# Releasing the next batch's work every fifteenth attention step instead of every step

## The reference

```python
xn = _layernorm(x, axis=-1)
q1 = (xn @ W1_q.T).reshape(B, T, H, 4); q2 = (xn @ W2_q.T).reshape(B, T, H, 4)
L_q = exterior(q1, q2)            # 6 normalized 2x2 minors for each head
L_k = exterior(k1, k2)            # the same of the keys
scores = jnp.einsum('bqhc,bkhc->bhqk', L_q, L_k @ _J6.T) * 6.0 ** (-0.5)
attn = jax.nn.softmax(jnp.where(causal, scores, -jnp.inf), axis=-1)
v = (xn @ W_v.T + b_v).reshape(B, T, H, 64)
out = jnp.einsum('bhqk,bkhd->bqhd', attn, v).reshape(B, T, D) @ W_out.T + b_out
out_real = xn_real @ W_real.T - xn_imag @ W_imag.T + bias_real
out_imag = xn_real @ W_imag.T + xn_imag @ W_real.T + bias_imag
return x + out + jnp.concatenate([out_real, out_imag], axis=-1)
```

## Time and profile before

| | |
|---|---|
| median of 3 runs | 4868.14 us (4857.08 to 4872.81) |
| the profiled execution | 4846.63 us, span of its slowest core 4845.6 us |
| spans of the 8 cores | 4806.8 to 4845.6 us |
| mean granted PE clock, core 7 | 0.658 of full speed |
| busy: PE, DVE, ACT | 59%, 29%, 30% of the span |

### The profile page before, as it was taken

The page is one execution under the profiler, slowest core; times in us unless marked ns, Lnnn a source line. Parts: engine busy times, 40 slices in busy tenths (PEclk is TensorE's granted clock), DMA queues, the critical chain, the costliest instruction groups (busy, mean ns, idle before and its releaser), DMA issues.

```text
span 4845.6 us, 35963 instructions; the slowest of 8 cores (4806.8 to 4845.6 us)
## 1 busy us (share of the span) xinstructions
PE 2867.5 (59%) x10528; PEld 980.5 (20%) x10528; DVE 1386.8 (29%) x2833; ACT 1474.5 (30%) x1729; POOL 129.4 (3%) x194
## 2 busy tenths in 40 slices
PE   1136655556665855556665675546665586666665
PEld 0113311112111511112111331112221151111112
DVE  0543433332222323332222323333232231111111
ACT  0000034443333014443332104443433203455450
POOL 3000000000000000000000010000000000000001
PEclk9986865557665875556765795555775596555558
DMA  7200311111200040111210041111210022000004
GB/s 78 49 26 1 106 53 31 29 38 65 66 22 11 14 70 27 29 31 57 69 41 9 7 64 33 33 31 38 70 64 11 5 32 45 14 14 11 14 11 72
DMA packets 88680, 180.26 MB, mean 37 GB/s; under 512 B 41760, under 2 KB 44968, under 8 KB 88496
## 3 DMA queue, kind: packets, MB, share of 16 engines
q0 software_dynamic: 55904, 73.28, 8.1%
q1 hardware_dynamic: 32592, 104.68, 7.4%
HBM read 114.36 MB, written 69.73 MB: 38 GB/s over the span
## 4 chain that ended last, share of the span: by engine, by line
PE 43%; DMA 22%; DVE 14%; ACT 11%; issue 7%; POOL 1%; DVEq 0%; SPq 0%; ACTq 0%; POOLq 0%
PE O L547 18%; DMA cdiv<-rscr 10%; DMA y<-ost 7%; PE S L507 7%; PE F L383 5%; ACT exps L530 4%; PE F L416 3%; DVE oT L585 3%; DMA rscr<-cdiv 3%; ACT cdiv L569 3%; ACT cdiv L567 3%; PE F L423 2%; PE F L309 2%; DVE exps L538 1%; DVE stat L267 1%
## 5 line engine op out<-in xcount | busy, mean ns | idle before, releaser
L530 ACT ACTIVATE exps<-S 128x1024 bf16<-128x1024 f32 (+3 forms) x1280 | 1120.0, 893 | 2099.4 <-PE O L547 1366.7
L547 PE MATMUL O<-exps,vaug 128*65 128x512 bf16 (+3 forms) x2560 | 1054.3, 513 | 840.6 <-DVE oT L585 500.8
L507 PE MATMUL S<-fqp,fkp 6*128 6x512 bf16 (+3 forms) x2560 | 625.2, 497 | 421.4 <-ACT exps L530 414.8
L547 PEld LDWEIGHTS O<-exps,vaug 128*65 128x65 bf16 x2560 | 232.9, 137 | 1290.1 <-issue 1271.1
L585 DVE TENSOR_TENSOR oT<-O,cdiv 64x512 bf16<-64x512 f32 x256 | 175.0, 683 | 922.5 <-DMA cdiv<-rscr 915.0
L507 PEld LDWEIGHTS S<-fqp,fkp 6*128 6x128 bf16 x2560 | 141.3, 97 | 1149.7 <-issue 1143.0
L538 DVE TENSOR_TENSOR exps<-exps,tri 128x256 bf16<-128x256 bf16 x512 | 143.2, 290 | 748.3 <-ACT exps L530 746.2
L456 PE MATMUL S<-wout,oT 128*128 128x512 bf16 x1024 | 254.4, 409 | 92.2 <-DVE ost L465 82.9
L383 PE MATMUL F<-wv,xnT 128*128 128x256 bf16 x2048 | 245.8, 278 | 0.8 <-DVE vaug L395 0.7
L295 PE MATMUL F<-idt,xnst 128*128 128x128 f32 x512 | 122.4, 419 | 175.2 <-DVE xnst L282 175.2
L383 PEld LDWEIGHTS F<-wv,xnT 128*128 128x128 bf16 x2048 | 187.8, 99 | 64.0 <-issue 30.7
(11 more groups left out here) (71 smaller groups left out, 1940.0 us busy)
## 6 DMA issues: line engine op xcount, KB each, us to landing
y<-ost POOLq DMA_DIRECT2D x128, 512.0 KB, 5.2
xst<-x SPq DMA_DIRECT2D x64, 512.0 KB, 4.3
x2st<-x SPq DMA_DIRECT2D x64, 512.0 KB, 4.1
cdiv<-rscr SPq DMA_DIRECT2D x128, 256.0 KB, 3.7
wv<-wvT POOLq DMA_DIRECT2D x8, 256.0 KB, 18.3
wout<-woutT POOLq DMA_DIRECT2D x8, 256.0 KB, 19.1
tascr<-qk SPq DMA_DIRECT2D x16, 128.0 KB, 1.7
rscr<-cdiv SPq DMA_DIRECT2D x128, 4.0 KB
```

The lines of the kernel that those rows point to most:

```text
L507: tS.inc(TE.matmul(S_ps[:, ss * 1024 + j * 512 + soff: ss * 1024 + j * 512 + 512], fk_pad[32 * m4:32 * m4 + 6, kt * 128:kt * 128 + 128], f ...
L530: sS.inc(SE.activation(e_out, e_in, AF.Exp))
L547: ins = TE.matmul(O4[:, j * 512 + off:(j + 1) * 512], vaug[:, kt * 1040 + h * 65: kt * 1040 + h * 65 + 65], exp_sb[:, ss * 1024 + j * 512 ...
```

## The change

`pace()` still counts every step, but returns at once unless the count is a multiple of 15. The target, when it is looked at, is the same function of the step as before, so the same items come in the same order, 2 or 3 (in the first half up to 4) at a time.

```diff
             def pace():
                 state["step"] += 1
+                if state["step"] % 15 != 0:
+                    return
                 target = state["step"] * total_items / 320.0
                 while state["popped"] < target:
```

## The result

The change makes the kernel slower: 5045.7 us (median of 10 runs, 5040.4 to 5053.3) against 4851.3 us (10 runs of the kernel before beside them). The ratio is 1.040, with a 95% interval of 1.038 to 1.042. Measured again beside the experiments it gave 1.041 (1.039 to 1.043). The forecast was 5033 us, in a range of 4950 to 5095.

The account below looks back on a forecast made before the run. No engine is near full, so order and waits bound the kernel. Parts of 91 + 107 + 82 = 280 us per batch against 231, taken as 55 more, three times: 165 on 4846.6, 5012, plus 21.5: 5033 us, range 4950 to 5095.

Parts of the forecast that it names:

- Second items wait uncovered: In a bunch nothing covers the second item's waits: 10.3 us from L282 to L282, 12.8 for two tiles ahead of masks.
- after a window's first step: Steps 45 and 105, two tiles: DVE comes straight from the division, first L282 5.3 late; 18.1 us each.
- one tile ahead of the masks: Steps 30 and 150: transposes must wait for L282 where they had not before; 2.5 us each.
- behind a mask: Step 90, one tile behind a mask: 8.8 us.
- at a last step: Step 120, one tile: L275 and L277 stand ahead of L567 on ACT and delay the division by 4.4 us.
- steps 15 and 135: Two tiles ahead of the masks, first L282 0.13 us after L547; priced at 12.8 us each.
- the clock behind transposes: First half, steps 15 to 150: transposes lift the PE clock now and then, as before; minus 5 us per batch.
- FFN: Second half, steps 165 to 270: bunches of n cost 4.5 + 7.55(n - 1) ahead of masks, less clock gain; sum 107 us.
- B bunches: Third part, steps 285, 300 and 315: B1 at 7.2, B2 at 14.9 or, last in a bunch, 12.3; sum 82 us.
- The clock rival: Every bunch, tiles included, leaves the clock up until the next division: 25 us per batch, 4943 us; chance 0.08.
- The divisions take the bunches: The cover of the divisions takes the bunches, so no change: 4868 us; chance 0.03.
- the rule that I weighed: Skill's rule that densely issued matmuls stay at full clock, so bunching should pay; weighed as holding only partly, for FFN bunches.

Follow-up runs that it names:

- run every tenth step: The change with items looked at every tenth step instead of every fifteenth, one whole tile at a time; 1.0152 of the kernel before.
- bunches at last steps: The change with the same 21 bunches, each moved to the nearest last step of a window; 1.0208 of the kernel before.
- run with two buffers: The change with loads of x alternating between xstage and x2stage; 1.0392 of the kernel before, against 1.0407 for the change.
- run with filled waits: The change with 16 extra unused matmuls on PE before the second tile's transposes in the five two-tile bunches; 1.0402 of the kernel before.
- last part alone: The change with only steps 267 to 320 bunched (B chunks), earlier steps taking items one by one; 1.0064 of the kernel before.
- table kernel: Items placed by a table of steps instead of a rate, without V tiles; 0.9305 of the kernel before, 336 us under it.

## Why the prediction was right

The step from single items to bunches held in kind and nearly in size. The forecast was +55 us per batch, or +165 in all, and +69 and +194 were measured. That the forecast of 5033 us comes within 13 us of the measured 5045.7 is in part luck: it started from 4868 us, and ten runs put the kernel before at 4851.3. For the three parts, on the slowest core's first batch, I had 432, 344 and 196 us; they took 442.8, 348.0 and 198.0. The 14 us per batch that are missing are made of the terms marked below (4, 4.5 and 3 us) and of 3.5 us in the start: I read the old cost of 231 us from one core's first batch, and the mean is 227.7.

- *Second items wait uncovered.* Forecast 10.3 us from L282 to L282 and 12.8 for two tiles; measured 10.13, and 12.8 at step 75 (mean of three batches). In the same mean, after a window's first step 18.1 against 17.8, one tile ahead of the masks 2.5 against 2.5, behind a mask 8.8 against 8.7, at a last step 4.4 against 4.4. The run every tenth step and the bunches at last steps confirm it with the same prices in other orders. The wording was partly wrong: I put the load first, and the run with two buffers shows that it is worth 0.6 of the 10 us.
- *Mis-sized: steps 15 and 135.* I priced both as "ahead of the masks", 12.8, with DVE's part done. They stand three steps behind the division, and these steps cover 3 of the 5.4 us that A1 takes to L282. In the trace ACT idles 2.15 us before the first L275, and each bunch cost 14.9: 4 us per batch.
- *Mis-sized: the clock behind transposes.* I took off 5 us as before, without asking what had lifted the clock. The bunches' part was at 0.50, and the steps without items gained 0.6 us (before, 8.5). This is 4.5 us of the miss.
- *FFN.* Forecast 107 with what the clock gives, about 110 measured; every bunch within 1.2 us in the mean (195: 19.6 against 18.5; 240: 12.9 against 12.5), and for the clock 11 forecast against 10. *Mis-sized: B bunches.* Steps 285 to 315 came to 85 instead of 82, 3 us.
- *Rivals.* The clock rival needed more than 0.52 in the first part; it went to 0.50. The run with filled waits shows that it is worth 7 us where it comes up behind half of the bunches. The prediction had the clock as something that bunches might win; it is 19 of the 69 us that they lose. "The divisions take the bunches" is refuted for everything with an ACT part, by the bunches at last steps; of two FFN the division covered 6 of 14 us.

On the rule that I weighed: the five steps behind the filled wait ran at a higher clock, 0.81 instead of 0.50. This agrees with what the Trainium skill (TensorE: Matmul & The Clock Gate, "Loop structure matters more than you think") says of dense matmuls, though the clock rose behind only half of the filled bunches. But bunching items whose parts wait for each other made no dense stretch: the first part's clock went down, from 0.55 to 0.50 in the mean.

## What to carry to other kernels

When background work is put between the steps of a loop with in-order engines, price each item by place, not by amount: how long has its first engine been free, which engines stand behind its waits, and what is next in their order. A bunch costs little only if its second item has nothing to wait for from the first. Ask too what the items' matmuls did for the clock of the steps between them: here that was 19 of 69 us. Idle time at a dependency covers work that is done on the dependency's engines before it needs them (one FFN, 0.3 us; of two, 7.7 were left); work that puts one wait ahead of it on its own engine delays it by its whole chain (4.4 us for a tile, 12.6 for B2).

## What the runs showed of the hardware

In the profiled execution of the change, the four cores of one die had a granted clock of 0.81 for 170 to 243 us of their span, and the other die's had none. A second FFN at step 240 runs in such a stretch (columns as above, PE clock 0.81):

```profile
1330.74:1334.90 4.16, 4.16 (x16) 1.74 (x17) 0.69 (x1) 0.00 (x0) 0.53 (x1) 0.81 0.79 253
```

Its 16 matmuls take 4.16 us. The die's median span was 5032.8 us against 5015.4 on the other; before, the two differed by 3. The second measurement's profile of the change has no such stretch. The run with filled waits had it on its first die, for 300 to 393 us, and the 0.81 in its last row above is this level. The run with the last part alone had it on both dies, for 96 to 427 us, and the table kernel on two of the first die's four cores only, for 63 and 73 us.

The Trainium skill (TensorE: Matmul & The Clock Gate, Part 1) describes a 13/16 clock for a whole die once three of its cores run dense matmuls. The level agrees (0.8125), and in the change so does the die; the two lone cores of the table kernel do not fit it, though the traces don't say what the other two ran at that moment. Why it came in some executions and not in others the runs do not show.

The change's loss does not hang on it: in the mean, the die without it took 438.3, 341.0 and 196.7 us for the three parts, the other 439.7, 343.6 and 196.9.
